# Last cross-attention of a two-layer decoder: values and a block of ones as the stationary operand

## The chip, the cores and the metric

One core of a Trainium2 chip runs the whole kernel in one launch. The metric is the device time of that launch in microseconds, as the median of several runs; lower is better. Everything is computed in 32-bit floats; operands declared F32R (fp32r) go through TensorE in one pass, plain F32 operands are issued as two matmul instructions each.

## The reference, cut to what matters

A decoder with two layers over x of shape (4, 512, 128) and a context of (4, 77, 128). Five blocks come before the one that is changed, one after it. The changed one is the last cross-attention:

```python
# _L1_xattn_ref(ctx, latents=x, ...): 16 heads of width 64, INNER = 1024
# media = layernorm(ctx) * w + b ; lat = layernorm(x) * w + b
# q = lat @ Wq + bq                          (4, 512, 1024)
# k, v = split(concat(lat, media) @ Wkv + bkv) (4, 589, 1024) each
# out = softmax(q k^T / 8) v, heads joined, @ Wout + bout
x = _layernorm(x + _L1_xattn_ref(ctx_1024, x, ...), axis=-1)
```

(The fence above is a summary in the reference's names.) For each of 4 batches and 16 heads there are 512 queries and 589 keys.

## The kernel before

The kernel is written engine by engine: each engine (sync, gpsimd, scalar, vector, tensor) has its own instruction list in a fixed order, and semaphores join them. Nothing is reordered at run time, so an instruction that waits holds up all that stands behind it on its engine.

The last cross-attention goes in 32 steps, one for a pair of heads `p` (`b, hp = divmod(p, 8)`). The 589 keys are five blocks `j` (four of 128 and one of 77), so a step has ten slots: five key blocks for head h = 0, then five for h = 1. In each slot TensorE issues, in this order:

1. `s_wide(p, slot)`: the scores of one key block, keys on the partitions and 512 queries in the free dimension, as two fp32r matmuls (high part, and the rest with the maxima's row).
2. `max_unit(p + 1, u)`: units of the row maxima of the next pair (slots 0 to 5 have 1, 2, 2, 2, 1, 2 of them); a unit is one matmul of 512 columns, every fifth is four of 78 columns. They alternate between two PSUM banks, so unit g waits until VectorE's `maxima` has reduced unit g - 2 (`mu_free`).
3. `pv(g - 1)`: the weighted values of the slot before. ScalarE has written the exponentials to `PX` (keys on partitions, 512 queries). Here `PX` is the stationary operand, one tile of 128 queries at a time, and the values `VXA` (64 columns and a column of ones) move; the result has queries on the partitions, and its 65th column is the sum for the quotient.
4. the tasks of that slot (`step_tasks`): Q and K of pair p + 2 (slots 0 and 3), Kt, the keys from the context (slot 5), `c`, the transposed maxima (slot 6), value products V of the next batch (slots 2 and 7 of the batch's first five steps), `oT` (slot 8), and `yE`, the output product of a batch (slot 9 of the next batch's first step). Tasks alternate between two PSUM banks; task n waits until task n - 2 has been read out (`pj_free`).

ScalarE does in each slot the exponential and then the high halves (`hi`) of Q, K and Kt. VectorE does in each slot, in this order: the reductions of the units; `head_out` of the last head in slot 0 and of this pair's first head in slot 5; the low halves (`lo`, which free the bank of Q, K or Kt); the other tasks (V copies, `c_rows`, the `oT` copy, `yE`). The first half of K's low part comes in slot 4, the second in slot 5, both parts of Kt in slot 6. `c_rows` hands the row of maxima to SyncE, which copies it by DMA into the `QB` operand of the next pair.

`head_out` takes the reciprocal of the four sums per partition, multiplies (128x256), and writes to `CT`; task `oT` then turns the pair with four transposes through ident, and VectorE copies the result to `OT`, which has the head's width on the partitions and queries in the free dimension, as the output product wants it.

The values are in two buffers by batch, `VXA[:, b % 2, j, head, :]`. All ten value products of batch 0 (five key blocks, two halves of 8 heads each) are in the prologue; those of a later batch are done in the batch before. GpSimd sets the columns of ones before the stage, ahead of the last two splits of the weights (`split_wide(5)`, `split_wide(6)`), on which the value products wait.

Of the kernel before, what the change touches and what calls it, by code (L numbers as in the profile page):

```python
# [159 lines left out]
def step_tasks(p):  # L160

    t = {}
    if p + 2 < PAIRS:
        t[0], t[3], t[5] = [("Q", p + 2)], [("K", p + 2)], [("Kt", p + 2)]
    if p + 1 < PAIRS:
        t[6] = [("c", p + 1)]
    b, hp = divmod(p, NHP)
    if b + 1 < B and hp < KB:
        t[2] = [("V", b + 1, 2 * hp)]
        t[7] = [("V", b + 1, 2 * hp + 1)]  # L170
    if p:
        t[8] = [("oT", p - 1)]
    if b and hp == 0:
        t[9] = [("yE", b - 1)]
    return t


def splits(tasks, slot):
# [5 lines left out]

PROLOGUE = ([("norm", 0), ("Q", 0), ("K", 0), ("Kt", 0), ("latT", 1), ("norm", 1), ("norm", 2), ("V", 0, 0), ("V", 0, 1),
             ("max", 0), ("max", 1), ("norm", 3), ("V", 0, 2), ("max", 2), ("max", 3), ("norm", 4), ("V", 0, 3), ("max", 4),
             ("max", 5), ("norm", 5), ("latT", 2), ("V", 0, 4), ("max", 6), ("max", 7), ("V", 0, 5), ("max", 8),
             ("max", 9), ("c", 0), ("Q", 1), ("V", 0, 6), ("K", 1), ("latT", 3), ("V", 0, 7), ("Kt", 1), ("V", 0, 8), ("V", 0, 9)])  # L190
EPILOGUE = [("oT", PAIRS - 1), ("yE", B - 1)]


def proj_tasks():
# [11 lines left out]
def decoder(nc, x, ctx, wq0, bq0, wk0, bk0, wv0, bv0, wo0, bo0, w_router, w_g, w_u, w_d, s_g, s_u, s_d, w_qkv,  # L206
# [3 lines left out]
    with es:  # L210
        def sb(name, shape, dt=F32):
            return es.enter_context(nc.sbuf_tensor(name, shape, dt))
# [81 lines left out]
        mxt = sb("mxt", [P, 2, 2, NT])  # L294
        cmx = sb("cmx", [P, 2, 2, NT])
        crow = sb("crow", [2 * NT, 2, P])
        rden = sb("rden", [P, 2, NT])

        vxa_at = nc.sbuf_base
        VXA = sb("VXA", [P, 2, KB, NH, DW + 1])  # L300
# [46 lines left out]

        LAT, LATT = Y, XT
        PX = BIG[:, 0:2048].rearrange("p (r n) -> p r n", r=4)
        CT = BIG[:, 2048:2048 + 2 * NT * P].rearrange("p (r t n) -> p r t n", r=2, t=NT)  # L350
        OT = REG[:, 0:NHP * S].rearrange("p (c n) -> p c n", c=NHP)
        wkv1s = REG[:, 6400 - 2 * INNER:6400]

# [110 lines left out]
        def _(pool):  # L464
# [128 lines left out]
            for key in D_NORMS:  # L593
                if key == ("D", 3):
                    split_lat(0)
                    split_wide(3)
                    split_wide(4)
                rstd(key)
                if key == ("D", 3):
                    pool.wait_ge(v_full, LV["kv", B - 1] + 1)  # L600
                    settled(pool.memset(VXA[:, :, :, :, DW:DW + 1], 1.0))
                    split_wide(5)
                    split_wide(6)
                elif key == ("lat", 2):
                    split_lat(1)
# [253 lines left out]
        def _(dve):  # L859
# [352 lines left out]
            def value(key):  # L1212
                _, b, u = key
                n = PJ[key]
                j, half = divmod(u, 2)
                rows = min(P, KEYS - P * j)
                if b == 0 and u == 0:
                    dve.wait_ge(setup_done, N_E_OPERANDS)
                dve.wait_ge(pj_full, n + 1)
                dve.tensor_copy(VXA[0:rows, b % 2, j, 8 * half:8 * half + 8, 0:DW],  # L1220
                                PS[0:rows, 6 + n % 2, :].rearrange("p (h d) -> p h d", h=8)).then_inc(pj_free, 1)

            def c_rows(key):
                p = key[1]
# [6 lines left out]
            def task(key):  # L1231
                kind = key[0]
                n = PJ[key]
                if kind == "V":
                    value(key)
                elif kind == "c":
                    c_rows(key)
                elif kind == "oT":
                    dve.wait_ge(pj_full, n + 1)
                    dve.tensor_copy(OT[:, key[1] % NHP, :], PS[:, 6 + n % 2, :]).then_inc(pj_free, 1)  # L1240
                else:
                    b = key[1]
# [17 lines left out]
            def head_out(head):  # L1260

                p, h = divmod(head, 2)
                b = p // NHP
                o = PS[:, 4 + head % 2, 0:NT * (DW + 1)].rearrange("p (t d) -> p t d", t=NT)
                dve.wait_ge(pv_ready, KB * (head + 1))
                link(dve.reciprocal(rden[:, head % 2, :], o[:, :, DW]))
                if p >= 2:
                    dve.wait_ge(pj_full, PJ["oT", p - 2] + 1)
                dve.tensor_tensor(CT[:, p % 2, :, DW * h:DW * h + DW], o[:, :, 0:DW],
                                  rden[:, head % 2, :].unsqueeze(2).broadcast_to([P, NT, DW]), ALU.mult).then_inc(on_ready, 1)  # L1270

            for key in PROLOGUE:
                if key[0] == "max":
# [31 lines left out]
                        if key[0] not in ("Q", "K", "Kt"):  # L1305
                            task(key)
            head_out(2 * PAIRS - 1)
            task(EPILOGUE[0])

            dve.wait_ge(cn_in, N_CN)  # L1310
            dve.tensor_scalar_mul(cbias[:, 0:1], cnb[:, 3:4], 0.5)
            dve.tensor_scalar_mul(cA[:], ar1[:], 0.3)
            dve.tensor_scalar_mul(cbias[:, 1:2], gnb[:, 2:3], 0.5).then_inc(coef_ready, 1)
            task(EPILOGUE[1])
            dve.wait_ge(pj_free, PJ["yE", B - 1] + 1)
            norm_stats(("E", B - 1), Y[:, B - 1])
            norm_apply(("E", B - 1), Y[:, B - 1], xtile("E", B - 1))
# [36 lines left out]
        def _(pe):  # L1354
# [342 lines left out]
            def task(key):  # L1697
# [5 lines left out]
                if kind in ("Q", "K", "Kt"):  # L1703
                    b, hp = divmod(key[1], NHP)
                    pe.wait_ge(latlo_ready, b + 1)
                    cols = slice(P * hp, P * hp + P)
                    if kind == "Q":
                        ins = product(bank, WQHI[:, cols], WQLO[:, cols], LATHI[:, b, :], LATLO[:, b, :])
                    elif kind == "K":
                        ins = product(bank, WKVHI[:, cols], WKVLO[:, cols], LATHI[:, b, :], LATLO[:, b, :])  # L1710
                    else:
                        ins = product(bank[:, 0:KEYS_PAD - S], WKVHI[:, cols], WKVLO[:, cols], MEDHI[:, b, :], MEDLO[:, b, :])
                elif kind == "V":
                    _, b, u = key
                    pe.wait_ge(latlo_ready, b + 1)
                    pe.wait_ge(wide_lo, 7)
                    j, half = divmod(u, 2)
                    cols = slice(INNER + 512 * half, INNER + 512 * half + 512)
                    rows = min(P, KEYS - P * j)
                    hi, lo = (LATHI[:, b, P * j:P * j + P], LATLO[:, b, P * j:P * j + P]) if j < NT else (MEDHI[:, b, 0:CK], MEDLO[:, b, 0:CK])  # L1720
                    ins = product(bank[0:rows, :], hi, lo, WKVHI[:, cols], WKVLO[:, cols])
                elif kind == "c":
                    p = key[1]
                    pe.wait_ge(cm_ready, 2 * (p + 1))
                    ins = pe.transpose(bank[0:2 * NT, 0:P], cmx[:, p % 2].rearrange("p h t -> p (h t)"), ident[:])
                elif kind == "oT":
                    p = key[1]
                    pe.wait_ge(on_ready, 2 * (p + 1))
                    for t in range(NT):
                        ins = pe.transpose(bank[:, P * t:P * t + P], CT[:, p % 2, t, :], ident[:])  # L1730
# [118 lines left out]
```

## Time and profile before

| what | value |
|---|---|
| median of 3 runs | 1247.82 us (1247.13 to 1249.44) |
| profiled execution, first to last instruction | 1246.1 us |
| what lies around that span, by the median | 1.7 us |
| mean granted TensorE clock | 0.937 of full speed |
| busy: PE / PEld / DVE | 1139.7 / 956.8 / 767.0 us |
| busy: ACT / POOL | 601.9 / 159.1 us |
| first score matmul of the changed stage | at 515.35 us |
| last value matmul of the stage ends | at 1160.9 us |

PE is TensorE's matmul, PEld its weight load, DVE VectorE, ACT ScalarE, POOL GpSimd. The profiled execution's own time is known only as this span, and the rows below are measured in it. The granted clock is given as a share of 2.4 GHz: 1.00 is that level, 0.50 is 1.2 GHz. A line of the profile can be that of a helper: all matmuls stand at L1368, so rows are told apart by the operands' names, and a tile that lies over another has the name of the space (BIG is `PX` or `CT`, VXA the values, REG `OT`).

### The profile page before, as it was taken

The page shows a single profiled execution, that of the slowest core. Times are in us where ns is not written, and L with a number is a line of the kernel's source. Part 1 is how long each engine was busy: PE and PEld are TensorE (multiplying, and loading weights), DVE is VectorE, ACT ScalarE, POOL GpSimd, SP SyncE. Part 2 cuts the span into 40 slices and gives each one's busy share as a digit, 9 for nine tenths or more (in the row PEclk, how much of TensorE's full clock was granted, in tenths as well). Part 3 has the DMA queues.
Part 4 walks back from the last instruction along what each step waited for, and adds up shares of the span by engine and source line. Part 5 has one row for each costly group of instructions (what it writes and reads, how often), then busy time and mean ns, then how long its engine had stood idle before and what let it go on. Part 6 is the DMA issues. An engine that isn't in the chain of part 4 may idle for free.

```text
span 1246.1 us, 18545 instructions
## 1 busy us (share of the span) xinstructions
PE 1139.7 (91%) x7050; PEld 956.8 (77%) x7050; DVE 767.0 (62%) x1794; ACT 601.9 (48%) x1096; POOL 159.1 (13%) x117
## 2 busy tenths in 40 slices
PE   7749999989999856799999999999999999999896
PEld 4537888978888744688888988889888889889632
DVE  5774556475565677657666567665867656664247
ACT  4213232433333444556565556564656565664353
POOL 6130000120733614200000000000000000000001
PEclk9878878789999976799999999999999999999998
DMA  6000000000000100000000000000000000000001
GB/s 211 0 1 1 1 1 1 1 1 1 1 1 1 34 0 1 1 2 1 1 2 1 1 2 1 1 2 1 1 1 1 2 1 1 2 1 1 1 0 34
DMA packets 10550, 9.97 MB, mean 8 GB/s; under 512 B 3627, under 2 KB 9695, under 8 KB 9951
## 3 DMA queue, kind: packets, MB, share of 16 engines
q1 hardware_dynamic: 10463, 8.79, 2.2%
q8 instruction: 57, 0.93, 0.3%
q14 instruction: 30, 0.25, 0.1%
HBM read 7.60 MB, written 1.05 MB: 7 GB/s over the span
## 4 chain that ended last, share of the span: by engine, by line
PE 71%; ACT 14%; DVE 9%; issue 5%; POOL 0%; DMA 0%; POOLq 0%; DVEq 0%; ACTq 0%
PE PS L1368 66%; ACT KA L814 8%; ACT BIG L831 4%; PE PS L1380 4%; DVE X_ODD L882 1%; PE PS L1730 1%; DVE st L871 1%; DVE REG L904 1%; DVE X_EVEN L882 1%; DVE mv L874 0%; DVE mxm L1253 0%; ACT BIG L639 0%; DVE Y L918 0%; DVE Y L882 0%; DVE VXA L1220 0%
## 5 line engine op out<-in xcount | busy, mean ns | idle before, releaser
L1368 PEld LDWEIGHTS PS<-VXA,BIG 128*128 128x128 f32 (+1 forms) x3136 | 397.0, 192 | 47.6 <-ACT BIG L831 23.7
L1368 PE MATMUL PS<-VXA,BIG 128*128 128x65 f32 (+2 forms) x3136 | 399.3, 272 | 9.2 <-ACT BIG L831 9.2
L831 ACT ACTIVATE BIG<-PS 128x512 f32<-128x512 f32 (+1 forms) x320 | 187.0, 594 | 178.7 <-PE PS L1368 175.8
L1253 DVE TENSOR_REDUCE mxm<-PS 128x1 f32<-128x512 f32 x256 | 170.7, 688 | 98.3 <-PE PS L1368 94.0
L814 ACT ACTIVATE KA<-PS,b1s 64x512 fp32r<-64x512 f32 (+1 forms) x256 | 128.5, 502 | 51.5 <-PE PS L1368 45.8
L1368 PE MATMUL PS<-QA,KA 128*128 128x512 f32 (+1 forms) x320 | 145.7, 455 | 0.0
L510 POOL TENSOR_TENSOR rs<-ve,half_neg 128x4 f32<-128x4 f32 (+1 forms) x29 | 30.3, 1047 | 888.2 <-DVE ve L876 888.2
L1368 PE MATMUL PS<-QB,KB 128*128 128x512 f32 (+1 forms) x320 | 126.2, 394 | 0.0
L1368 PE MATMUL PS<-KA,QA 128*128 128x512 f32 (+1 forms) x512 | 116.2, 331 | 2.8 <-DVE mxm L1253 2.6
L1368 PEld LDWEIGHTS PS<-KA,QA 128*128 128x128 f32 x512 | 87.0, 190 | 23.0 <-DVE mxm L1253 4.8
L736 ACT ACTIVATE BIG<-PS 128x512 f32<-128x512 f32 x72 | 42.3, 596 | 96.6 <-PE PS L1368 96.3
L1208 DVE SCALAR_TENSOR_TENSOR KB<-PS,b1s,KA 64x78 fp32r<-64x78 f32 (+1 forms) x128 | 67.0, 524 | 12.8 <-ACT KA L814 6.3
L1052 DVE TENSOR_TENSOR BIG<-PS,BIG 128x512 f32<-128x512 f32 x72 | 48.5, 689 | 40.5 <-PE PS L1368 23.0
L1368 PE MATMUL PS<-REG,VXA 128*128 128x462 f32 (+1 forms) x96 | 53.4, 711 | 17.7 <-DVE BIG L970 16.2
L581 POOL TENSOR_TENSOR VXA<-VXA,half_neg 128x128 f32<-128x128 f32 x3 | 62.2, 20727 | 49.3 <-DVE VXA L1058 49.3
L814 ACT ACTIVATE QA<-PS,b1s 64x512 fp32r<-64x512 f32 x64 | 43.7, 683 | 47.7 <-PE PS L1368 46.9
L1368 PE MATMUL PS<-XHI,UPHI 128*128 128x512 f32 x144 | 61.7, 428 | 5.1 <-DVE BIG L1052 4.5
L1368 PEld LDWEIGHTS PS<-v0x,BIG 77*128 77x128 f32 x512 | 64.0, 207 | 0.8 <-issue 0.8
L1368 PE MATMUL PS<-v0x,BIG 77*128 77x9 f32 x512 | 63.8, 266 | 0.8 <-DVE Y L987 0.8
L1368 PEld LDWEIGHTS PS<-QB,KB 128*128 128x128 f32 (+1 forms) x320 | 58.6, 183 | 5.5
L1368 PEld LDWEIGHTS PS<-QA,KA 128*128 128x128 f32 (+1 forms) x320 | 58.6, 183 | 4.4 <-issue 0.2
L1240 DVE COPY REG<-PS 128x512 f32<-128x512 f32 x32 | 22.1, 691 | 61.7 <-PE PS L1730 61.7
(250 smaller groups left out, 1683.8 us busy)
## 6 DMA issues: line engine op xcount, KB each, us to landing
X_EVEN<-in_x SPq DMA_DIRECT2D x4, 256.0 KB, 3.8
VXA<-in_L_ffn_Wg SPq DMA_DIRECT2D x1, 1024.0 KB, 5.7
VXA<-in_L_ffn_Wu SPq DMA_DIRECT2D x1, 1024.0 KB, 7.8
VXA<-in_L_ffn_Wd SPq DMA_DIRECT2D x1, 1024.0 KB, 9.4
REG<-in_L_xattn_Wkv SPq DMA_DIRECT2D x1, 1024.0 KB, 4.9
QB<-crow SPq DMA_DIRECT2D x64, 2.0 KB
out<-X_EVEN SPq DMA_DIRECT2D x4, 256.0 KB, 2.3
wq1s<-in_L_xattn_Wq SPq DMA_DIRECT2D x1, 512.0 KB, 8.6
```

Source lines behind the costliest of these rows:

```text
L510: pool.tensor_tensor(rs[0:rows, n, :], ve[0:rows, n, :], half_neg[0:rows, 0:NT], ALU.pow).then_inc(rstd_ready, 1)
L581: pool.tensor_tensor(SSQ[b], SSQ[b], half_neg[:, 0:1].broadcast_to([P, NSQ]), ALU.pow).then_inc(pow_ready, 1)
L736: act.activation(SG[:, n % 4, :], PS[:, n % 2, :], ACT.Silu).then_inc(silu_ready, 1)
L814: act.activation(dst, PS[own, 6 + n % 2, 0:width], ACT.Identity, bias=bias).then_inc(hi_ready, 1)
L831: act.activation(PX[0:rows, g % 4, :], PS[0:rows, g % 2, :], ACT.Exp, scale=SCALE_W).then_inc(pw_ready, 1)
L882: ins = dve.tensor_scalar(dst[0:rows, t, :], src[0:rows, t, :], mv[0:rows, n, t, 0:1], rs[0:rows, n, t:t + 1], ALU.subtract, ALU.mult)
L1052: dve.tensor_tensor(HX[:, e_all % 3, k, :], PS[:, 2 + n % 2, :], SG[:, n % 4, :], ALU.mult).then_inc(h_ready, 1)
L1208: ins = dve.scalar_tensor_tensor(dst, PS[rows, 6 + n % 2, 0:width], bias, lead.bitcast(F32), ALU.add, ALU.subtract)
L1240: dve.tensor_copy(OT[:, key[1] % NHP, :], PS[:, 6 + n % 2, :]).then_inc(pj_free, 1)
L1253: dve.tensor_reduce(mxm[:, p % 2, h, m:m + 1], PS[:, 2 + g % 2, :], AX.X, ALU.max).then_inc(mu_free, 1)
L1368: return pe.matmul(dst, lhsT, rhs, start=start, stop=stop, **kw)
L1380: ins = pe.transpose(bank[0:src.shape[1], rows * n:rows * n + rows], src, ident[0:rows, 0:rows])
```

## The change

The value product is turned. The exponentials (`PX`, 512 queries) move, and the stationary operand is a 128-column slice of a new layout `VV[rows, j, pair, 192]`: the values of the pair's first head, 64 columns of ones, the values of its second. For h = 0 the slice is values and ones, for h = 1 ones and values, so the head's result stands on its own 64 partitions and its sum, 64 times over, on the other 64. `head_out` takes the reciprocal of those 64x512, multiplies, and writes to `OT` directly; `CT`, the task `oT` and its copy go.

There is one value buffer. The half for pairs 4 to 7 of a batch is filled in slots 2 and 7 of that batch's own steps hp = 0 to 2, the half for pairs 0 to 3 of the next batch in steps hp = 4 to 6. The prologue keeps the five products of the first half. `yE` moves from slot 9 to slot 2 of the same step.

```diff
 def step_tasks(p):
-    if b + 1 < B and hp < KB:
-        t[2] = [("V", b + 1, 2 * hp)]
-        t[7] = [("V", b + 1, 2 * hp + 1)]
-    if p:
-        t[8] = [("oT", p - 1)]
+    half, step = 1 - hp // 4, hp % 4
+    owner = b + 1 - half
+    for slot, j in ((2, 2 * step), (7, 2 * step + 1)):
+        if owner < B and j < KB:
+            t[slot] = [("V", owner, 2 * j + half)]
     if b and hp == 0:
-        t[9] = [("yE", b - 1)]
+        t[2] = t[2] + [("yE", b - 1)]
...
-EPILOGUE = [("oT", PAIRS - 1), ("yE", B - 1)]
+EPILOGUE = [("yE", B - 1)]
...
+        rden = BIG[:, 2048:2048 + S]
+        VV = vflat[:, 0:KB * NHP * 3 * DW].rearrange("p (j c d) -> p j c d", j=KB, c=NHP)
+        VH = vflat[:, 0:KB * NHP * 3 * DW].rearrange("p (j c h d) -> p j c h d", j=KB, c=NHP, h=3)
...
-                    settled(pool.memset(VXA[:, :, :, :, DW:DW + 1], 1.0))
+                    settled(pool.memset(VV[:, :, :, DW:2 * DW], 1.0))
...
-                dve.tensor_copy(VXA[0:rows, b % 2, j, 8 * half:8 * half + 8, 0:DW],
-                                PS[0:rows, 6 + n % 2, :].rearrange("p (h d) -> p h d", h=8)).then_inc(pj_free, 1)
+                dve.tensor_copy(VH[0:rows, j, 4 * half:4 * half + 4, 0:3:2, :],
+                                PS[0:rows, 6 + n % 2, :].rearrange("p (c h d) -> p c h d", c=4, h=2)).then_inc(pj_free, 1)
...
-                o = PS[:, 4 + head % 2, 0:NT * (DW + 1)].rearrange("p (t d) -> p t d", t=NT)
+                own, other = slice(DW * h, DW * h + DW), slice(DW * (1 - h), DW * (1 - h) + DW)
                 dve.wait_ge(pv_ready, KB * (head + 1))
-                link(dve.reciprocal(rden[:, head % 2, :], o[:, :, DW]))
-                if p >= 2:
-                    dve.wait_ge(pj_full, PJ["oT", p - 2] + 1)
-                dve.tensor_tensor(CT[:, p % 2, :, DW * h:DW * h + DW], o[:, :, 0:DW],
-                                  rden[:, head % 2, :].unsqueeze(2).broadcast_to([P, NT, DW]), ALU.mult).then_inc(on_ready, 1)
+                link(dve.reciprocal(rden[own, :], PS[other, 4 + h, :]))
+                if h == 0 and p and p % NHP == 0:
+                    dve.wait_ge(pj_full, PJ["yE", b - 1] + 1)
+                dve.tensor_tensor(OT[own, p % NHP, :], PS[own, 4 + h, :], rden[own, :], ALU.mult).then_inc(on_ready, 1)
...
-                for t in range(NT):
-
-                    ins = mm(PS[:, 4 + head % 2, (DW + 1) * t:(DW + 1) * (t + 1)], PX[0:rows, g % 4, P * t:P * t + P],
-                             VXA[0:rows, b % 2, j, 2 * hp + h, :], start=j == 0 and t == 0, stop=j == KB - 1, skip_group_check=True)
+                at = DW * h
+                ins = mm(PS[:, 4 + h, :], VV[0:rows, j, hp, at:at + 2 * DW], PX[0:rows, g % 4, :], start=j == 0, stop=j == KB - 1)
```

The prologue's list loses ("V", 0, 1), ("V", 0, 3), ("V", 0, 5), ("V", 0, 7) and ("V", 0, 9).

## Rows read from the trace of the kernel before

**Rows 1.** The page's chain that ended last, shares of the span by line.

```profile
PE PS L1368 66%; ACT KA L814 8%; ACT BIG L831 4%; PE PS L1380 4%; DVE X_ODD L882 1%; PE PS L1730 1%; DVE st L871 1%; DVE REG L904 1%; DVE X_EVEN L882 1%; DVE mv L874 0%; DVE mxm L1253 0%; ACT BIG L639 0%; DVE Y L918 0%; DVE Y L882 0%; DVE VXA L1220 0%
```

**Rows 2.** Windows: stretch, us, busy PE PEld DVE ACT POOL, PEclk, DMA.

```profile
576.61:597.05 20.44, 20.12 (x138) 17.84 (x138) 13.51 (x26) 12.26 (x22) 0.00 (x0) 1.00 0.01 1
636.52:655.60 19.08, 18.76 (x133) 16.75 (x132) 12.23 (x24) 12.27 (x22) 0.00 (x0) 1.00 0.01 2
```

**Rows 3.** TensorE in order of time: start, us, operation [idle before <-releaser].

```profile
588.11 0.76 PE L1368 MATMUL PS<-KA,QA 128*128 128x512 f32 x5
588.70 1.09 PE L1368 MATMUL PS<-VXA,BIG 77*128 77x65 f32 x8
589.59 0.28 PE L1368 MATMUL PS<-MEDHI,WKVHI 128*128 128x78 f32 x1
...
589.93 0.48 PE L1368 MATMUL PS<-QA,KA 128*128 128x512 f32 x1
590.25 0.39 PE L1368 MATMUL PS<-QB,KB 128*128 128x512 f32 x1
590.48 1.00 PE L1368 MATMUL PS<-VXA,BIG 128*128 128x65 f32 x8
591.32 0.27 PE L1725 MATMUL PS<-ident,cmx 128*8 128x128 f32 x1
...
592.36 1.11 PE L1368 MATMUL PS<-VXA,BIG 128*128 128x65 f32 x8 [0.32 <-ACT BIG L831]
...
595.36 0.60 PE L1730 MATMUL PS<-ident,BIG 128*128 128x128 f32 x4
595.72 0.47 PE L1368 MATMUL PS<-QA,KA 128*77 128x512 f32 x1
...
1161.73 0.63 PE L1730 MATMUL PS<-ident,BIG 128*128 128x128 f32 x4 [0.82 <-DVE BIG L1269]
```

**Rows 4.** TensorE in order of time, last stage, plain f32 products.

```profile
1211.05 1.02 PE L1368 MATMUL PS<-BIG,cn 128*128 128x512 f32 x2
1211.90 1.02 PE L1368 MATMUL PS<-XT,twist 128*128 128x512 f32 x2
```

**Rows 5.** VectorE's groups by shape: count, busy us, mean ns, idle before.

```profile
L1133 DVE RECIPROCAL eq<-PS 128x32 f32<-128x32 f32 x8 | 2.8, 355 | 5.9 <-PE PS L1368 5.6
...
L1208 DVE SCALAR_TENSOR_TENSOR KB<-PS,b1s,KA 64x512 fp32r<-64x512 f32 x64 | 48.0, 749 | 5.9 <-ACT KA L814 3.8
...
L1245 DVE TENSOR_TENSOR Y<-PS,X_EVEN 128x512 f32<-128x512 f32 x4 | 2.8, 692 | 31.6 <-PE PS L1368 31.6
...
L1266 DVE RECIPROCAL rden<-PS 128x4 f32<-128x4 f32 x64 | 11.7, 183 | 14.3 <-PE PS L1368 9.8
...
L986 DVE RECIPROCAL r<-PS 128x16 f32<-128x16 f32 x16 | 4.1, 258 | 23.2 <-PE PS L1368 23.2
```

**Rows 6.** VectorE in order of time, slot 5 of the same step.

```profile
589.15 0.47 DVE L1255 TENSOR_REDUCE mxt<-PS 128x4 f32<-128x312 f32 x1
589.65 0.16 DVE L1258 TENSOR_TENSOR cmx<-mxm,mxt 128x4 f32<-128x4 f32 x1
...
590.04 0.42 DVE L1269 TENSOR_TENSOR BIG<-PS,rden 128x256 f32<-128x256 f32 x1
```

**Rows 7.** Windows of the prologue of the stage, columns as in rows 2.

```profile
487.30:490.80 3.50, 2.75 (x9) 1.34 (x8) 3.46 (x12) 0.00 (x0) 1.25 (x2) 0.97 0.00 0
490.80:494.10 3.30, 1.39 (x7) 0.82 (x7) 3.27 (x11) 0.00 (x0) 1.01 (x1) 1.00 0.00 0
494.10:497.60 3.50, 3.50 (x11) 2.88 (x12) 3.47 (x8) 1.41 (x2) 1.18 (x1) 0.53 0.00 0
497.60:501.10 3.50, 1.62 (x7) 0.71 (x5) 3.50 (x7) 0.00 (x0) 0.10 (x1) 0.98 0.00 0
...
511.30:518.10 6.80, 6.40 (x16) 4.38 (x17) 3.35 (x6) 3.80 (x7) 6.08 (x5) 0.50 0.00 0
```

**Rows 8.** GpSimd in order of time, the columns of ones.

```profile
477.13 0.38 POOL L601 MEMSET VXA<- 128x160 f32 x1
```

More of the change, by code:

```diff
@@ L182, in splits @@
             + [(key, 1) for key, _ in now if key[0] == "Kt"])
[L187 to L190, printed above, removed]
-EPILOGUE = [("oT", PAIRS - 1), ("yE", B - 1)]
+PROLOGUE = ([("norm", 0), ("Q", 0), ("K", 0), ("Kt", 0), ("latT", 1), ("norm", 1), ("norm", 2), ("V", 0, 0),
+             ("max", 0), ("max", 1), ("norm", 3), ("V", 0, 2), ("max", 2), ("max", 3), ("norm", 4), ("max", 4),
+             ("max", 5), ("norm", 5), ("latT", 2), ("V", 0, 4), ("max", 6), ("max", 7), ("max", 8),
+             ("max", 9), ("c", 0), ("Q", 1), ("V", 0, 6), ("K", 1), ("latT", 3), ("Kt", 1), ("V", 0, 8)])
+EPILOGUE = [("yE", B - 1)]
 def proj_tasks():
@@ L296, in decoder @@
         crow = sb("crow", [2 * NT, 2, P])
-        rden = sb("rden", [P, 2, NT])
         vxa_at = nc.sbuf_base
@@ L349, in decoder @@
         PX = BIG[:, 0:2048].rearrange("p (r n) -> p r n", r=4)
-        CT = BIG[:, 2048:2048 + 2 * NT * P].rearrange("p (r t n) -> p r t n", r=2, t=NT)
+        rden = BIG[:, 2048:2048 + S]
+        VV = vflat[:, 0:KB * NHP * 3 * DW].rearrange("p (j c d) -> p j c d", j=KB, c=NHP)
+        VH = vflat[:, 0:KB * NHP * 3 * DW].rearrange("p (j c h d) -> p j c h d", j=KB, c=NHP, h=3)
         OT = REG[:, 0:NHP * S].rearrange("p (c n) -> p c n", c=NHP)
@@ L1237, in task @@
                     c_rows(key)
-                elif kind == "oT":
-                    dve.wait_ge(pj_full, n + 1)
-                    dve.tensor_copy(OT[:, key[1] % NHP, :], PS[:, 6 + n % 2, :]).then_inc(pj_free, 1)
                 else:
@@ L1307, in _ @@
             head_out(2 * PAIRS - 1)
-            task(EPILOGUE[0])
             dve.wait_ge(cn_in, N_CN)
@@ L1313, in _ @@
             dve.tensor_scalar_mul(cbias[:, 1:2], gnb[:, 2:3], 0.5).then_inc(coef_ready, 1)
-            task(EPILOGUE[1])
+            task(EPILOGUE[0])
             dve.wait_ge(pj_free, PJ["yE", B - 1] + 1)
@@ L1672, in pv @@
                     pe.wait_ge(on_ready, head - 1)
-                if j == 0 and hp == 0 and h == 0:
-                    pe.wait_ge(pj_free, PJ["V", b, 2 * KB - 1] + 1)
-                for t in range(NT):
-                    ins = mm(PS[:, 4 + head % 2, (DW + 1) * t:(DW + 1) * (t + 1)], PX[0:rows, g % 4, P * t:P * t + P],
-                             VXA[0:rows, b % 2, j, 2 * hp + h, :], start=j == 0 and t == 0, stop=j == KB - 1, skip_group_check=True)
+                if j == 0 and hp % 4 == 0 and h == 0:
+                    pe.wait_ge(pj_free, PJ["V", b, 2 * (KB - 1) + hp // 4] + 1)
+                at = DW * h
+                ins = mm(PS[:, 4 + h, :], VV[0:rows, j, hp, at:at + 2 * DW], PX[0:rows, g % 4, :], start=j == 0, stop=j == KB - 1)
                 ins.then_inc(pv_ready, 1)
@@ L1725, in task @@
                     ins = pe.transpose(bank[0:2 * NT, 0:P], cmx[:, p % 2].rearrange("p h t -> p (h t)"), ident[:])
[L1726 to L1730, printed above, removed]
                 else:
                     b = key[1]
-                    pe.wait_ge(pj_free, PJ["oT", NHP * b + NHP - 1] + 1)
+                    pe.wait_ge(on_ready, 2 * NHP * (b + 1))
                     for t in range(NT):
@@ L1759, in _ @@
             pv(SLOTS * STEPS - 1)
-            task(EPILOGUE[0])
             def input_f(b):
@@ L1769, in _ @@
                 input_f(b)
-            task(EPILOGUE[1])
+            task(EPILOGUE[0])
             pe.wait_ge(cn_in, N_CN)
```

## The prediction

> **What bounds the kernel now.** I read the page's chain first. TensorE carries it, by far the largest part on the helper line of the matmuls, and the exponentials and high-half evictions of ScalarE come next [rows 1]. Then the stretches: one step of the last cross-attention, from its first score matmul to that of the next step, takes 20.44 us where two value products are in it and 19.08 us where none is, so a value product costs (20.44 - 19.08) / 2 = 0.68 us. TensorE is busy for all but 0.32 us of either, VectorE for 13.5 and 12.2 us, ScalarE for 12.3 us [rows 2]. So TensorE is the bound of these 32 steps and VectorE has about 7 us to spare in each. Third, TensorE in order of time [rows 3] and VectorE beside it [rows 6], because what matters is not the sum of VectorE's work but where it stands in the queue. Fourth, the granted clock where TensorE has to wait, which in this kernel is the prologue of the stage [rows 7].
>
> **TensorE's own work.** The change swaps 8 short matmuls in a slot (four tiles of 65 columns, each issued twice) for one product with 512 columns, issued twice. Today one slot's value matmuls take from 590.48 to 591.32, 0.84 us, elsewhere 0.81 to 0.89; the score pair ahead of them takes from 589.93 to 590.48, 0.55 us [rows 3]. The form that comes in stands at the end of the kernel: a plain f32 product of 128x512 takes from 1211.05 to 1211.90, 0.86 us with rounding [rows 4]. I take 0.86. What is gained is in the neighbour: after a 65-column matmul the first score matmul waits for its weights (0.32 to the next one, where the second takes 0.23), and behind a 512-column matmul that load is covered, so a score pair costs 2 x 0.23 = 0.46. A slot of score and value goes from about 1.36 to 1.32. Ten slots give back 0.4 us. The four transposes of oT go: 595.36 to 595.72, 0.36 us a step [rows 3]. Counted form by form, a step with two value products then has 10 x 0.46 for scores, 10 x 0.86 for values, 8 x 0.23 and 2 x 0.36 for the maxima units, 4 x 0.69 for Q, K and V, 0.34 for Kt (589.59 to 589.93), and some 0.2 for exposed loads around Kt and c: 19.1 us of work. If the rest of the chip kept up, that would be 1.3 us less than the 20.44 of today, 0.3 of which is the wait for the exponential that 592.36 shows.
>
> **VectorE's new work.** Today a head costs a reciprocal of 128x4 (0.18, [rows 5]) and a product of 128x256 (0.42, [rows 6]), and a pair the copy for oT. After it each head has a reciprocal of 64x512 and a product of 64x512. The product is bounded by the 128x512 rows: 0.69. For the reciprocal three sizes are in the trace: 4 elements 183 ns, 16 elements 258 ns, 32 elements 355 ns [rows 5]. The slopes are 6.25 and 6.06 ns per element; an ordinary operation has (692 - 160) / 508 = 1.05, from 128x512 and the 0.16 of a 128x4 one [rows 5, 6]. At 6.1 ns the reciprocal is 0.183 + 508 x 0.0061 = 3.28 us. Bounds from both sides: 0.69, if 512 elements streamed like a copy, and 3.28 by the slope. I take 3.28: three points lie on one line, though 512 is sixteen times the largest. A head's output is then 3.28 + 0.03 + 0.69 = 4.0 us instead of 0.6. The Trainium skill, "VectorE: DVE Perf Modes", section "First, the fixed hardware budget", says that reciprocal runs an iterative divide with a repeat count of 8. The trace agrees that it is several times dearer, at 6.1 / 1.05 = 5.8 element times and not 8.
>
> **Where that stands in the queue.** VectorE's sum per step becomes 13.5 - 1.2 - 0.7 + 8.0 = 19.6 us, just over TensorE's 19.1, but the order costs more than the sum. Both head outputs stand ahead of work for which TensorE has little else to do.
>
> Stall A, slot 0. head_out(2p-1) stands ahead of the reductions of units 1 and 2, and TensorE has two banks for units: unit 3 waits for unit 1's reduction. From the end of TensorE's last value matmul: 0.2 drain (it is 1.00 long where the next begins 0.8 later), 4.0 head output, 0.69 reduction, 0.05 to wake: 4.95. TensorE has meanwhile Q 0.69, a score 0.46, units 1 and 2 0.46, a value product 0.86, a score 0.46 = 2.93. It waits 2.02, issues unit 3 (0.23), and waits 0.45 more for unit 2's reduction. Together 2.47.
>
> Stall B, slot 5. head_out(2p) stands ahead of the second low half of K, and task c in slot 6 uses the bank which that frees. Counted from stall A, VectorE reaches head_out after 7 reductions (4.83), two tails (0.47 + 0.16 each [rows 6]), three low halves at 0.75 [rows 5] and a V copy at 0.69, with 0.5 of waiting: 13.85; TensorE has ended the head's last value product at 13.5. So 0.35 + 4.0 + 0.75 + 0.05 = 5.15 until c may go, against Kt 0.34 + score 0.46 + value 0.86 = 1.66. Stall 3.5 us. ScalarE is done by then (its last exponential ends at about 14.2). Behind c stand the scores of slot 7 and everything after it; VectorE's own idle time at the step's end, some 4 us, can't be used, because the next reduction waits for the next step's unit 0.
>
> A step is 19.1 + 2.47 + 3.5 = 25.0 us with two value products (before 20.44), and 23.6 with none (before 19.08): +4.55. The first 30 of the 32 steps have both the Q/K work and the maxima: 136.5. c is issued some 4.8 us before the next step's first score, where it had 5.7 (591.32 to 597.05), and SyncE's DMA of its row has that time to land: I take it as hidden, and if the difference were missing it would cost 0.9 us a step.
>
> **Smaller terms.** Value products: 30 in the steps before, 35 after, 5 x 0.68 = +3.4. The prologue loses five: three lie in the stretch where VectorE is busy throughout (3.27 of 3.3, 3.47 of 3.5, 3.50 of 3.5 us, [rows 7]) and give 3 x 0.6, the last stands alone ahead of the first score and gives 1.5: -3.3. yE in slot 2 waits for Q's late low half, 0.9 x 3 = +2.7; its length is as before. The first step has no stall A, the last two only the gain or stall A: -1.5. At the end 4.3 us until the transposes for the last stage may go instead of 0.82 [rows 3], less 0.46 of oT: +3.0. The ones: Pool's memset of 160 elements took 0.38 us [rows 8]; 2560 elements at up to 0.85 ns add at most 2 us, behind which the last split ends at 482.0, and the first value product begins at 483.8: nothing. Without that cover, up to 2. Sum: 136.5 + 3.4 - 3.3 + 2.7 - 1.5 + 3.0 = +140.8.
>
> **The clock.** This is the largest choice. Both steps shown ran at a granted clock of 1.00, 2.4 GHz [rows 2], as all of them did. In the prologue, where TensorE was busy 1.39 of 3.3 us, and again 1.62 of 3.5, the clock was 1.00 in that stretch and 0.53 or less in the next; with 2.75 of 3.5 busy it stayed. At the lower level of 1.2 GHz TensorE then worked for 3.3 to 3.5 us, three times (494.1 to 497.6 is shown), and once for 6.8 (511.3 to 518.1) before the clock rose [rows 7]. Mean of the four 4.3 us at half speed: 2.15 us lost per fall. Stall B leaves TensorE idle for 3.5 us, stall A for 2.47 of 2.7. The work behind both is bound by TensorE, so the loss is in full on the path. I take a fall at each B (30 x 2.15 = 64.5) and at four in five of A (51.6), less 0.15 x 30 because a slower TensorE meets a readier VectorE: +112. The Trainium skill, "TensorE: Matmul & The Clock Gate", section "HAM oscillation — how this bites in real kernels", describes a loop whose every pass starts at the lower level after its wait; the prologue's rows agree, and no row of the steps can.
>
> **The number.** Against the profiled span: 1246.1 + 140.8 + 112 = 1499. The median of the runs is 1.7 us over that span: 1500 us.
>
> **Rivals.**
> 1. The clock stays at 2.4 GHz through stalls of 2.5 and 3.5 us. For: the steps have dense work between the stalls. Against: the prologue. 1246.1 + 140.8 + 1.7 = 1389 us.
> 2. Faster: the long reciprocal streams. At 0.69 us stall A is gone (2.36 against 2.93), stall B is 2.56 - 1.66 = 0.9. A step is 19.1 + 0.9 = 20.0, -0.46 x 30 = -14; with value products, prologue and ends -15: 1233 us. It decides at a reciprocal of about 1.15 us, where stall B alone (reciprocal + 0.2) eats the 1.35 us that TensorE gains: 2 ns per element. Against: 6.1 in three rows.
> 3. The reciprocal takes eight element times at length: 0.16 + 512 x 8 x 1.05 ns = 4.5 us. Both stalls grow by 1.2: 30 x 2.4 + 1.2 = +73, 1573 us. Against: the slope. This is the size that the repeat count of that page of the Trainium skill would give.
> 4. Each fall lasts 6.8 us, not 4.3: 60 x 3.4 = 204 in place of 112: 1592 us. One row of four.
>
> **Chances.** My forecast with its clock falls 0.70; rival 1 0.14; rival 2 0.04; rival 3 0.05; rival 4 0.06; no change, were the stalls to cancel the gains, 0.01. 0.2% is what a measurement here can tell. Faster 0.04, same 0.01, slower 0.95. The range goes down to rival 1's 1389, rounded to 1385, and up to 1580, between rivals 3 and 4.
>
> **What would show it.** Value matmuls: 640 of 512 columns, 0.43 us apart. The reciprocal of 64x512 near 3.3 us. Waits of TensorE in slot 2 on a reduction (L1253's line) near 2 us, and in slot 6 on K's low half near 3.5. VectorE at or over 75% busy in the steps. Granted clock of the steps 0.75 to 0.85; 1.00 would mean rival 1. It would be wrong if the reciprocal's cost doesn't grow with its elements, or if something else stands ahead of c.

## The result and the profile after

The changed kernel takes 1501.17 us (median of 4 runs, 1498.11 to 1503.32) against 1247.63 of the kernel before in the same comparison: ratio 1.2018, 95% interval 1.1993 to 1.2044. The profiled execution spans 1498.8 us, against a forecast of 1499 for it.

The page's chain, shares by line; it answers to [rows 1].

```profile
PE PS L1364 63%; DVE BIG L1264 14%; PE PS L1376 3%; DVE mxm L1251 3%; DVE KB L1209 2%; DVE REG L1267 2%; DVE X_ODD L883 1%; DVE st L872 1%; PE PS L1719 1%; DVE REG L905 1%; DVE X_EVEN L883 1%; ACT KA L815 0%; DVE mv L875 0%; ACT BIG L640 0%; DVE Y L919 0%
```

Before, no line of VectorE had more than 1%. Now one, the reciprocal (L1264), has 14% of the span. Its groups by shape, with count, busy us, mean ns and idle before; they answer to [rows 5]:

```profile
L1264 DVE RECIPROCAL BIG<-PS 64x512 f32<-64x512 f32 x64 | 214.7, 3355 | 14.7 <-PE PS L1364 13.7
L1267 DVE TENSOR_TENSOR REG<-PS,BIG 64x512 f32<-64x512 f32 x64 | 44.1, 689 | 2.2
```

TensorE in order of time in one step with two value products, which answers to [rows 3] (the rows of neighbouring matmuls overlap, and the one behind a value product is given an early start, so spacings are best taken between rows of the same kind: 592.91 to 594.23, one slot of score and value, is 1.32 us):

```profile
592.91 0.39 PE L1364 MATMUL PS<-QB,KB 128*77 128x512 f32 x1
...
594.23 0.39 PE L1364 MATMUL PS<-QB,KB 128*128 128x512 f32 x1
...
598.27 0.40 PE L1364 MATMUL PS<-QB,KB 128*128 128x512 f32 x1
600.62 1.24 PE L1364 MATMUL PS<-KA,QA 128*128 128x512 f32 x5 [1.95 <-DVE mxm L1251]
601.68 1.77 PE L1364 MATMUL PS<-BIG,VXA 128*128 128x512 f32 x2
...
608.75 0.77 PE L1364 MATMUL PS<-KA,QA 128*128 128x512 f32 x5
609.34 1.10 PE L1364 MATMUL PS<-BIG,VXA 77*128 77x512 f32 x2
...
611.08 1.08 PE L1364 MATMUL PS<-BIG,VXA 128*128 128x512 f32 x2
615.41 0.27 PE L1719 MATMUL PS<-ident,cmx 128*8 128x128 f32 x1 [3.24 <-DVE KB L1209]
```

and VectorE beside it, which answers to [rows 6]:

```profile
595.76 3.35 DVE L1264 RECIPROCAL BIG<-PS 64x512 f32<-64x512 f32 x1 [0.17 <-PE PS L1364]
599.15 0.69 DVE L1267 TENSOR_TENSOR REG<-PS,BIG 64x512 f32<-64x512 f32 x1
599.87 1.29 DVE L1251 TENSOR_REDUCE mxm<-PS 128x1 f32<-128x512 f32 x2
...
610.49 3.36 DVE L1264 RECIPROCAL BIG<-PS 64x512 f32<-64x512 f32 x1
613.88 0.68 DVE L1267 TENSOR_TENSOR REG<-PS,BIG 64x512 f32<-64x512 f32 x1
614.60 1.40 DVE L1209 SCALAR_TENSOR_TENSOR KB<-PS,b1s,KA 64x512 fp32r<-64x512 f32 x3
```

The two fences are read together. The unit that TensorE starts at 600.62 could go when the first of the two reductions from 599.87 was done, and that one stood behind the head output from 595.76 to 599.84. The transpose of the maxima (task c) at 615.41 could go when K's second low half, first of the three operations from 614.60, was done; it stood behind the head output from 610.49 on.

The row of five matmuls at 600.62 is unit 3 and the four matmuls of unit 4. A wait for unit 2's reduction lies inside it, and TensorE's weight loads show it:

```profile
601.22 0.52 PEld L1364 LDWEIGHTS PS<-KA,QA 128*128 128x128 f32 x4 [0.41 <-DVE mxm L1251]
```

From 600.62 to the value product at 601.68 are 1.06 us; the same five at 608.75, with no wait, take 0.59 to 609.34. So unit 4 waits 0.47 us. Over the stage, TensorE's waits for VectorE, in us in total, times, longest:

```profile
PE PS L1719 <- DVE KB L1209: 97.5, 30, 3.3
PE PS L1364 <- DVE mxm L1251: 59.1, 30, 2.6
```

Last the windows, columns as in [rows 2]: 29 steps (from the task c of the first step to that of the thirtieth), then pieces of the step above. 1.00 is 2.4 GHz.

```profile
531.98:1366.34 834.36, 680.92 (x2208) 412.99 (x2208) 566.77 (x744) 358.78 (x638) 3.03 (x3) 0.87 0.00 1
...
592.30:600.00 7.70, 6.37 (x22) 3.65 (x20) 4.87 (x4) 5.01 (x9) 0.00 (x0) 1.00 0.00 0
600.30:601.70 1.40, 0.99 (x6) 0.67 (x6) 1.37 (x3) 0.00 (x0) 0.00 (x0) 1.00 0.00 0
600.30:604.00 3.70, 3.29 (x9) 1.91 (x10) 3.59 (x7) 0.00 (x0) 0.00 (x0) 0.73 0.00 0
...
615.40:619.00 3.60, 3.59 (x8) 2.16 (x9) 0.86 (x3) 0.60 (x1) 0.00 (x0) 0.53 0.00 1
```

The same 29 steps of the kernel before:

```profile
530.37:1124.11 593.74, 584.85 (x4048) 522.21 (x4048) 381.96 (x767) 355.64 (x639) 3.03 (x3) 1.00 0.01 1
```

So 834.36 - 593.74 = 240.6 of the 252.7 us are in these 29 steps. The clock was 1.00 up to the first wait and still 1.00 for the units right behind it; then it fell, 0.73 over the stretch from 600.30 to 604.00 and 0.53 behind the second wait.

### The profile page after: what moved, and what is told of

Its sections match the earlier page's. It is cut to its first block, busy times and chain, and to the rows that moved or that the text cites. A ratio compares the mean times of both kernels' runs of the same rounds, so it can differ in the third digit from the quotient of the medians.

```text
span 1498.8 us, 14328 instructions
## 1 busy us (share of the span) xinstructions
PE 1238.4 (83%) x5002; PEld 831.5 (55%) x5002; DVE 966.2 (64%) x1762; ACT 605.2 (40%) x1096; POOL 160.8 (11%) x117
## 3 DMA queue, kind: packets, MB, share of 16 engines
HBM read 7.60 MB, written 1.05 MB: 6 GB/s over the span
## 4 chain that ended last, share of the span: by engine, by line
PE 67%; DVE 26%; issue 3%; ACT 2%; POOL 0%; DMA 0%; POOLq 0%; DVEq 0%; SPq 0%; ACTq 0%
PE PS L1364 63%; DVE BIG L1264 14%; PE PS L1376 3%; DVE mxm L1251 3%; DVE KB L1209 2%; DVE REG L1267 2%; DVE X_ODD L883 1%; DVE st L872 1%; PE PS L1719 1%; DVE REG L905 1%; DVE X_EVEN L883 1%; ACT KA L815 0%; DVE mv L875 0%; ACT BIG L640 0%; DVE Y L919 0%
## 5 line engine op out<-in xcount | busy, mean ns | idle before, releaser
L1364 PE MATMUL PS<-BIG,VXA 128*128 128x512 f32 (+1 forms) x640 | 386.5, 690 | 0.0
L1264 DVE RECIPROCAL BIG<-PS 64x512 f32<-64x512 f32 x64 | 214.7, 3355 | 14.7 <-PE PS L1364 13.7
L1364 PE MATMUL PS<-QA,KA 128*128 128x512 f32 (+1 forms) x320 | 223.1, 697 | 1.2 <-DMA QB<-crow 1.2
L1364 PE MATMUL PS<-KA,QA 128*128 128x512 f32 (+1 forms) x512 | 137.3, 366 | 65.7 <-DVE mxm L1251 62.8
L1364 PEld LDWEIGHTS PS<-BIG,VXA 128*128 128x128 f32 (+1 forms) x640 | 131.0, 217 | 34.0 <-ACT BIG L832 7.3
L1364 PE MATMUL PS<-QB,KB 128*128 128x512 f32 (+1 forms) x320 | 138.7, 434 | 0.0
L1364 PEld LDWEIGHTS PS<-QA,KA 128*128 128x128 f32 (+1 forms) x320 | 67.6, 211 | 55.6 <-issue 36.8
L1719 PE MATMUL PS<-ident,cmx 128*8 128x128 f32 x32 | 11.0, 343 | 98.3 <-DVE KB L1209 97.5
L1364 PEld LDWEIGHTS PS<-VXA,BIG 128*128 128x128 f32 x576 | 69.7, 191 | 3.2
L1364 PE MATMUL PS<-REG,VXA 128*128 128x462 f32 (+1 forms) x96 | 56.4, 745 | 18.1 <-DVE BIG L971 16.5
L1364 PE MATMUL PS<-VXA,BIG 128*128 128x128 f32 x576 | 69.9, 275 | 0.0
```

Of the source, the lines that this page charges most:

```text
L1264: link(dve.reciprocal(rden[own, :], PS[other, 4 + h, :]))
L1364: return pe.matmul(dst, lhsT, rhs, start=start, stop=stop, **kw)
```

## The experiments

### e1: a copy in place of the reciprocal

```diff
-                link(dve.reciprocal(rden[own, :], PS[other, 4 + h, :]))
+                link(dve.tensor_copy(rden[own, :], PS[other, 4 + h, :]))
```

> The changed kernel with the reciprocal of 64x512 replaced by a copy of 64x512, so the quotient is left out and the values are multiplied by their sums. Theory (the long reciprocal in VectorE's queue is the whole cost): head output 0.69 + 0.03 + 0.69 = 1.4 us in place of 4.1, no wait at unit 3, about 0.9 us at c, the clock of the steps at 1.00, 1233 us (1225 to 1242), so below the kernel before. Rival (the turned product, the single value buffer or the moved yE cost by themselves): clearly over 1247, and in full 1501.

Measured: 1235.37 us, ratio to before 0.9903 (0.9871 to 0.9934). The group and TensorE's longest wait in its profile:

```profile
L1264 DVE COPY BIG<-PS 64x512 f32<-64x512 f32 x64 | 44.1, 688 | 21.1 <-PE PS L1364 20.1
```

```profile
PE PS L1719 <- DVE KB L1209: 17.6, 30, 0.6
```

The one instruction carries the whole loss. All other edits (turned product, one value buffer, yE in slot 2, no oT) together make the kernel 1% faster, as the theory had it. Its wait at c is 0.6 us where 0.9 was expected. Its 29 steps, with which the later ones are compared:

```profile
532.68:1119.43 586.75, 568.32 (x2209) 361.42 (x2210) 410.48 (x744) 358.75 (x639) 3.03 (x3) 1.00 0.00 1
```

### e2: the kernel before, with one more reciprocal

```diff
                 link(dve.reciprocal(rden[:, head % 2, :], o[:, :, DW]))
+                link(dve.reciprocal(spare[0:DW, :], ones[0:DW, 0:1].broadcast_to([DW, S])))
```

> The kernel before, with one more reciprocal of 64x512 (from a tile of ones into a spare tile) inside head_out, ahead of the multiplication; nothing else changed. Theory (waits and clock falls come from VectorE's queue, whatever the form of the value product): head output 0.18 + 3.35 + 0.42 = 3.95 us, the same two waits, of about 1.9 and 3.2 us, the same falls of the clock, and none of TensorE's gain of 0.8 us a step: 1515 us (1490 to 1540). Rival 1 (the turned 512-column products bring the clock down, not the waits): clock 1.00 in the steps, 1247 + 30 x 5.0 = 1397 us. Rival 2 (the turned product costs, not the reciprocal): under 1260 us.

Measured: 1574.4 us, ratio 1.2606 (1.2585 to 1.2627). That is above the range of the theory, and far from both rivals. The waits, and the 29 steps:

```profile
PE PS L1727 <- DVE KB L1209: 96.3, 30, 3.2
PE PS L1370 <- DVE mxm L1254: 51.1, 30, 2.4
```

```profile
536.39:1441.57 905.18, 761.38 (x4046) 667.94 (x4047) 574.74 (x825) 359.18 (x638) 3.03 (x3) 0.78 0.00 1
```

The waits are as expected, 147 us where the changed kernel has 157. So the cost of the queue doesn't need the turned product. What was missed is the clock: 0.78 against 0.87 with no more waiting. What that costs can be read from TensorE's busy time, for its matmuls are those of the kernel before: 761.38 - 584.85 = 177 us more in the 29 steps. Some 14 us of it are unit 4's wait, which lies inside a joined row (29 x 0.47), so about 163 us are the clock. The changed kernel against e1 in the same way: 680.92 - 568.32 - 14 = 99 us. (The span times what the clock lacks of 1.00, 905.18 x 0.22 = 199 and 834.36 x 0.13 = 108, gives more, for it takes every microsecond at the lower level as half lost.) The rival that the turned product brings the clock down is refuted with its sign turned: with the old form it stays down longer. Two stretches right behind a wait show it in one step, where the changed kernel is back at 1.00 by 605.5:

```profile
639.27:642.70 3.43, 3.33 (x15) 2.84 (x16) 3.29 (x6) 0.00 (x0) 0.00 (x0) 0.66 0.00 0
642.70:646.10 3.40, 3.40 (x12) 2.73 (x11) 1.92 (x3) 0.60 (x1) 0.00 (x0) 0.50 0.00 0
```

TensorE was busy throughout and still at 1.2 GHz. That the short 65-column matmuls are the reason is not shown: they are the main difference on TensorE between the two, but the four transposes of oT are there as well, and no run takes the two apart.

### e3: the waits filled with matmuls that nobody reads

```diff
+            def fill(g, count):
+                pe.wait_ge(latlo_ready, B)
+                pe.wait_ge(pw_ready, g)
+                for _ in range(count):
+                    mm(PS[:, (g + 1) % 2, :], WQHI[:, 0:P], LATHI[:, B - 1, :])
...
                     s_wide(p, slot)
+                    if slot == 2 and 0 < p < PAIRS - 1:
+                        fill(SLOTS * p + slot, 7)
...
+                    if slot == 6 and p < PAIRS - 2:
+                        fill(SLOTS * p + slot, 13)
```

> The changed kernel with matmuls that nobody reads in TensorE's two waits: 7 of 128x512 fp32r (1.6 us) ahead of unit 3 in slot 2, 13 (3.0 us) ahead of c in slot 6, into the score bank that the next slot overwrites. Theory (the falls of the clock come from TensorE standing still, and cost about 112 us): clock of the steps at or near 1.00, 1390 us (1375 to 1410), although TensorE has 4.6 us more to do in each step. Rival (the clock falls for another cause, or is cheap because the work behind is not bound by TensorE): 1501 us or more.

Measured: 1401.95 us, ratio 1.1231 (1.1199 to 1.1262): 99 us faster than the changed kernel with 20 more matmuls a step. The 29 steps:

```profile
532.98:1272.08 739.10, 717.26 (x2788) 468.25 (x2789) 565.15 (x744) 358.83 (x638) 3.03 (x3) 1.00 0.00 1
```

The clock is 1.00, and 834.36 - 739.10 = 95 us are the clock's part in the steps, close to the 99 from the busy times. The other part is the queue, less what TensorE gains: 739.10 - 593.74 = 145 us. TensorE still waits 10.5 us for reductions and 8.0 at c in all, so the filling was a little short of the waits and did not lengthen them. A step with two value products takes 25.24 us from one task c to the next, one without 23.85; the prediction had 25.0 and 23.6.

### e4: the first head's output later in the queue

```diff
-                    if slot == KB:
-                        head_out(2 * p)
...
+                    if slot == 7:
+                        head_out(2 * p)
```

> The changed kernel with head_out of the pair's first head moved in VectorE's queue from slot 5, ahead of K's second low half, to the end of slot 7, where VectorE had 4 us idle. Theory (order in the queue, not the sum of the work): the wait of 3.25 us at c goes in all 30 steps (-98 us) and with it the falls of the clock there (30 x 1.7 to 2.0, -55); some 0.5 us a step comes back at slot 0 because the output now ends late: 1364 us (1335 to 1390). Rival (the sum of VectorE's work is what bounds, 19.6 us and more a step): the waits only move to another place, 1480 to 1510 us.

Measured: 1375.58 us, ratio 1.102 (1.1001 to 1.1038), 126 us faster than the changed kernel where 137 were expected. Its waits and its 29 steps:

```profile
PE PS L1364 <- DVE mxm L1251: 76.7, 33, 3.0
PE PS L1364 <- ACT BIG L832: 9.3, 30, 0.3
```

```profile
528.86:1244.31 715.45, 628.44 (x2209) 380.90 (x2208) 565.04 (x743) 356.03 (x639) 3.03 (x3) 0.94 0.00 1
```

The wait at c is gone, all 97.5 us. The waits for reductions grew by 17.6, and the old wait for the exponential is back with 9.3. The clock's part, from the busy times as in e2, is 628.44 - 568.32 - 14 = 46 us, 53 less than in the changed kernel. -97.5 + 17.6 + 9.3 - 53 = -124, and -126 was measured. It is the same instruction with the same VectorE sum (565 against 567 us busy), only in another place, so order costs and not the sum.

### e5: one reciprocal for both heads, off the path

```diff
+            def take(head):
+                ...
+                act.activation(SD[own, p % 2, :], PS[other, 4 + h, :], ACT.Copy).then_inc(on_ready, 1)
+                act.activation(TV[own, p % 2, :], PS[own, 4 + h, :], ACT.Copy).then_inc(on_ready, 1)
...
-            def head_out(head):
+            def shares(p, parts):
+
+                dve.wait_ge(on_ready, 4 * (p + 1))
+                for c in parts:
+                    cols = slice(P * c, P * c + P)
+                    ins = dve.reciprocal(SD[:, p % 2, cols], SD[:, p % 2, cols])
+                if parts[-1] == NT - 1:
+                    link(ins)
+                    dve.tensor_tensor(OT[:, p % NHP, :], TV[:, p % 2, :], SD[:, p % 2, :], ALU.mult).then_inc(fin, 1)
...
+                    if p and slot in (6, 7, 8, 9):
+                        shares(p - 1, [slot - 6])
```

> The changed kernel with the quotient taken out of the path: ScalarE copies each finished head's values and sums from PSUM (two copies of 64x512, 0.68 us each), sums of both heads into one 128x512 tile, so that one reciprocal serves the pair. VectorE does it a step later in four pieces of 128 columns in slots 6 to 9, then one multiplication of 128x512 into OT; yE moves to slot 2 of the batch's second step. Theory (the value product itself saves TensorE 0.8 us a step and only the place and number of long reciprocals cost): VectorE has 4 x 0.95 + 0.69 = 4.5 us a pair where the changed kernel has 8.1, and nothing waits for them; ScalarE 15 us of 19.5; steps of 19.5 and 18.1 us, clock 1.00, 1222 us (1212 to 1235), below both kernels. Rival (VectorE and ScalarE have no room left once they carry the quotient and the copies): waits of TensorE for exponentials or reductions of 1 us or more a step, 1247 us or more.

Measured: 1240.31 us, ratio 0.9923 (0.9905 to 0.994): 0.8% faster than the kernel before, but 18 us slower than expected and outside the stated range. One piece of the reciprocal, its multiplication, and TensorE's wait:

```profile
L1279 DVE RECIPROCAL BIG<-BIG 128x128 f32<-128x128 f32 x128 | 110.5, 915 | 12.1 <-ACT VXA L826 11.2
L1282 DVE TENSOR_TENSOR REG<-VXA,BIG 128x512 f32<-128x512 f32 x32 | 22.2, 692 | 1.1
```

```profile
PE PS L1377 <- ACT BIG L843: 9.3, 30, 0.3
```

VectorE's part came as reckoned (4 x 0.915 + 0.69 a pair). The expectation left out a wait that the kernel before has too, the one for the exponential of slot 6, which stands behind four evictions of Kt on ScalarE. Steps take 19.8 and 18.4 us, where 19.5 and 18.1 were expected (some 9 us in all), and from the last task c to the end it is 110.1 us against 104.7 in the kernel before, for now the last pair's division stands alone there. The two make some 15 of the 18 us.

### e6: the same, with those two waits mended

```diff
                     for key, h in splits(tasks, slot):
-                        hi(key, h)
+                        if (key[0], h) != ("Kt", 1):
+                            hi(key, h)
+                    if slot == 6 and p + 2 < PAIRS:
+                        hi(("Kt", p + 2), 1)
...
-            shares(PAIRS - 1, [0, 1, 2, 3])
+            dve.wait_ge(on_ready, 4 * PAIRS)
+            for c in range(NT):
+                cols = slice(P * c, P * c + P)
+                last = (PAIRS - 1) % 2
+                link(dve.reciprocal(SD[:, last, cols], SD[:, last, cols]))
+                dve.tensor_tensor(OT[:, NHP - 1, cols], TV[:, last, cols], SD[:, last, cols], ALU.mult).then_inc(fin, 1)
...
+                        if b == B - 1 and t:
+                            pe.wait_ge(fin, PAIRS + t)
```

> The version with the shared reciprocal, with two waits mended that its trace shows. ScalarE evicts the second half of Kt behind the next exponential instead of ahead of it (TensorE waited 0.3 us in PE's rows, up to 0.5 between matmuls, for that exponential, in each of 30 steps), and the last pair is divided by query tiles of 128 columns, so that the last output product begins after the first of four pieces instead of after 3.4 + 0.7 us. Theory (these two are on the path): 30 x 0.35 + 2.5 = 13 us less than the 1240 us of the version before it: 1227 us (1222 to 1234). Rival (the exponential's wait moves to VectorE's reciprocals, which end 0.4 us before the next unit must be reduced): only the end's 2.5 us, 1238 us.

Measured: 1226.43 us, ratio 0.9813 (0.9789 to 0.9838), as expected in total. No wait for the exponential of a step is left among TensorE's; the 29 steps:

```profile
525.65:1101.33 575.68, 569.70 (x2209) 360.59 (x2208) 440.53 (x768) 426.15 (x755) 3.03 (x3) 1.00 0.00 1
```

The parts erred both ways: the steps gave 8 us (583.67 in e5) where 10.5 were expected, for three waits for a reduction grew from 1.0 to 4.4 us together, and the end gave 6 (103.9 from the last task c) where 2.5 were. This is the version to keep.

### e7 and e8: how long a reciprocal may be

```diff
-                link(dve.reciprocal(rden[own, :], PS[other, 4 + h, :]))
+                link(dve.reciprocal(rden[own, 0:160], PS[other, 4 + h, 0:160]))
```

and the same with 256.

> The changed kernel with the reciprocal taken over the first 160 of 512 columns alone; the other columns are multiplied by whatever stands in the tile, so the quotient is right for 160 queries only. Theory (the decisive length of about 1.15 us that the prediction named, above which the wait at c eats what TensorE gains): a reciprocal of 0.18 + 156 x 0.0062 = 1.15 us, no wait at unit 3, the wait at c 0.6 + 0.46 = 1.1 us, clock 1.00, 1235 + 30 x 0.46 = 1249 us (1243 to 1256), level with the kernel before. Rival (any reciprocal ahead of the reductions brings the clock down): over 1290 us.

> The changed kernel with the reciprocal taken over the first 256 of 512 columns alone, the rest left out in the same way. Theory: 0.18 + 252 x 0.0062 = 1.75 us, the wait at unit 3 0.5 and at unit 4 up to 0.4, the wait at c 1.7 us: 1235 + 30 x (1.06 + 0.7) = 1288 us (1275 to 1300) if the clock stays at 1.00, as it did in the prologue where TensorE stood still for 0.75 of 3.5 us. Rival (waits of 1.7 us bring the clock down already, as waits of 1.9 of 3.3 us did in the prologue): 50 us more, 1320 to 1350 us.

Measured: 1265.65 us with 160 columns, ratio 1.0121 (1.0087 to 1.0156), and 1306.08 with 256, ratio 1.0434 (1.0397 to 1.0471). Both are 17 to 18 us above the theory; the clock of the steps is 1.00 in both, so neither rival holds. The reciprocal in the two profiles, and TensorE's weight load waiting for a reduction in the first, which the expectation had at nothing:

```profile
L1264 DVE RECIPROCAL BIG<-PS 64x160 f32<-64x160 f32 x64 | 73.9, 1155 | 19.8 <-PE PS L1364 18.8
```

```profile
PEld PS L1364 <- DVE mxm L1251: 18.4, 60, 0.9
```

```profile
L1264 DVE RECIPROCAL BIG<-PS 64x256 f32<-64x256 f32 x64 | 112.3, 1755 | 18.0 <-PE PS L1364 17.0
```

TensorE's waits in the second, 1.65 and 0.37 us a step:

```profile
PE PS L1719 <- DVE KB L1209: 49.5, 30, 1.7
PE PS L1364 <- DVE mxm L1251: 11.1, 30, 1.0
```

The durations are right to 5 ns. The missing term is unit 4's wait for unit 2's reduction. It begins before unit 3's: with a reciprocal R, unit 4 can't go until R + 0.2 + 0.72 + 2 x 0.69 + 0.05 = R + 2.35, against a cover of 2.93 + 0.23 = 3.16, so from R = 0.81 on and not from 1.27. At 1.155 that is 0.34 us a step, besides 0.47 more at c. A step with two value products measures 20.00 us in e1 and 20.82 here: 0.82, which is that sum. In e8 it is 22.04, where the same reckoning gives 20.00 + 0.95 + 1.07 = 22.02. Over the steps this accounts for 10 of the 17 us in e7 and for 7 to 8 of the 18 in e8. The rest is in no wait that was found; e1, on whose 1235 us both sums stand, itself has runs from 1234.5 to 1243.0, and the profiled one took 1241.7. From 0.81 us on each further microsecond of reciprocal costs two a step, once at each head.

## Why the prediction was right

The total, 1500 against 1501.2, is better than its parts, which erred both ways.

- **TensorE's own work.** A slot of 1.32 us, which with scores of 0.23 leaves 0.43 for each value product: as predicted. A step of e6b with two value products takes 19.30 us from one task c to the next with no wait in it, where 19.1 was predicted and the kernel before has 20.44 less 0.32. That all this is a gain is shown by e1 (0.9903), which left the rest of the change in place. Rival 2 gave 1233 us for a reciprocal that streams; e1 is that case and took 1235.
- **The reciprocal.** 3.28 predicted from three points of at most 32 elements, 3.355 measured at 512; the slope held over sixteen times the largest size in the rows, which was a bet. At 6.24 ns per element against 1.05 it is 5.9 element times, not the eight of rival 3. Head output 4.0 predicted; 595.76 to 599.84 is 4.08.
- **Stall A.** 2.02 us at unit 3 predicted, 1.95 by TensorE's row, and 2.12 by starts (the score row at 598.27 and 0.23 for it, to 600.62). The further 0.45 at unit 4 is 0.47, inside the joined row at 600.62; e3, at the full clock, has the same.
- **Stall B.** 3.5 predicted; 3.24 by the row, 3.47 by starts (611.08 and 0.86 for the pair, to 615.41). The 0.35 us by which VectorE would come late to the head output was some 0.1, in the changed kernel and in e3 alike, so the lower clock is not the reason; the terms listed for it add up to 13.7 us and not 13.85. TensorE's cover, 1.74 us by starts, was as predicted (1.66).
- **The queue in all.** 140.8 us predicted. Measured at full clock in e3: 145 in 29 steps and some 10 ahead of and behind them in the profiles, 1401.95 - 1248.87 = 153 in the times. So this term was too small by about 12. A step with two value products is 25.24 us where 25.0 was predicted, which makes some 7 of it. The 3.3 us that the prologue was to give back can't be seen: its task c stands at 501.50 before and at 501.44 after, and in the runs with the same prologue anywhere from 500.56 to 505.93.
- **The clock.** 112 us predicted, 99 measured by e3 (95 in the 29 steps). So this was too large by 13, and the two errors cancel, which is luck. That falls come from TensorE standing still is shown: filling the waits took them all away. The prediction took 2.15 us for each of 54 falls; measured are 1.6 to 1.7 us for each of 58 waits in the changed kernel and some 2.8 in e2. So the price, taken from four stretches of the prologue, was near by luck in part: it says nothing of how it depends on the matmuls behind the wait.
- **Smaller terms.** From task c of the last step to the end is 109.9 us where the kernel before has 104.7, +5.1 against +3.0 at the end less the 0.8 that the last step's slots gain; the granted clock of that stretch is 0.93, before 0.96. The memset was hidden, as said, at 2.23 us:

```profile
478.86 2.23 POOL L602 MEMSET VXA<- 128x2560 f32 x1
```

- **Two signs that did not come out.** The clock of the steps was to be 0.75 to 0.85 and is 0.87; VectorE was to be busy 75% or more and is busy 566.77 of 834.36 us, 68%. Neither contradicts the mechanism: the prediction's own terms give a step of 25.0 + 112 / 30 = 28.7 us, hence 1 - 3.7 / 28.7 = 0.87 and 19.6 / 28.7 = 68%. The signs were not worked out from the sum.
- **The rivals.** Rival 1 (the clock stays) is e3 in effect: 1389 was its number, 1402 its measured one. Rivals 3 and 4 are refuted by 3.355 us and by the 0.87. Where the prediction was wrong is rival 2's point of decision, "about 1.15 us": at 1.155 the kernel is 1.2% slower already. Between e1 (0.9903 at 0.69) and e7 (1.0121 at 1.155) the ratio crosses 1 at about 0.9 us. The step that failed in it is the count of stall A by unit 3 alone.

What stays open: why the old form of the value product, with waits no longer, loses 163 us to the clock where the turned form loses 99.

## What to carry to other kernels

Before an operation is put into an engine's fixed queue, ask what stands right behind it and how much work the waiting engine has left: against the kernel before, the same 3.36 us cost 253 us here ahead of two releases and 127 ahead of one of them (e4), and once a step later, and serving two heads at once, the kernel was 0.8% faster (e5). An operation whose cost grows with its elements at another rate than its neighbours' must be priced by its own slope: the product got 0.8 us a step cheaper on TensorE, and gave its divisor 128 times as many elements in each partition. When the engine that sets the end stands still again and again, ask what the lower clock behind the waits costs as well; with waits of 1.95 and 3.24 us in every step it was two fifths of the loss here, with 1.7 and 0.4 (e8) nothing.

## What the runs showed of the hardware

- VectorE's reciprocal is linear over the whole range seen: 183 ns at 4 elements [rows 5], 915 at 128, 1155 at 160, 1755 at 256, 3355 at 512: (3355 - 183) / 508 = 6.24 ns per element. The lengths read from PSUM lie within 3 ns of that line, for 64 and for 128 partitions; 3345 ns at 512 from SBUF (e2) does within 10, and the 128-element pieces of e5, from SBUF and back to back, are 42 ns under it.
- Waits of 1.7 us and 0.4 us in each step left the clock at 1.00 (e8); waits of 1.95 and 3.24 us brought it to 0.87 over the steps.
- With 65-column value products TensorE was longer at 1.2 GHz behind its waits than with 512-column ones (e2: 0.78 over the steps, with 147 us of waits; the changed kernel: 0.87 with 157); why is open.
- 20 matmuls a step that nobody reads made the kernel 99 us faster (e3).
